# A cross-attention, attention and mixture-of-experts layer: the weight split moved into the second walk, the replicating loads cut in two halves by heads

## The reference

```python
def reference(x, ctx, ...):
    x = x + xattn(layernorm(x), ctx, Wq, bq, Wk, bk, Wv, bv, Wo, bo)
    return x + block(layernorm(x), ...)

def block(x):                                   # x: (8, 512, 256), float32
    q, k, v = heads(x @ wq), heads(x @ wk), heads(x @ wv)        # 16 heads of 16
    attn = softmax(causal(q @ k.T / 4))
    h = x + rmsnorm((attn @ v) @ wo, attn_norm_w)
    dense = h + rmsnorm((silu(h @ w1) * (h @ w3)) @ w2, ff_norm_w)
    probs = softmax(x @ router_w)
    topw, topi = top_k(probs, 2)
    sparse = rmsnorm(sum(topw * expert(topi, x)), moe_norm_w)
    return dense + sparse
```

## Time and profile before

| | us |
|---|---|
| median of three runs | 1455.98 (1455.1 to 1457.37) |
| the profiled execution | 1460.08 |
| its span | 1458.3 |
| PE busy | 1329.9 (91%) |
| DVE busy | 816.3 (56%) |
| ACT busy | 561.9 (39%) |
| POOL busy | 607.0 (42%) |
| mean granted TensorE clock | 0.969 |

### The profile page before, as it was taken

How to read it: one execution, slowest core, us unless ns; L and a number is a source line. 1 busy time by engine, 2 the same in 40 slices (tenths; PEclk the granted TensorE clock), 3 DMA queues, 4 the chain that set the end, 5 groups by cost and what they waited for, 6 DMA issues and landing times. The chain is left out here.

```text
span 1458.3 us, 21947 instructions
## 1 busy us (share of the span) xinstructions
PE 1329.9 (91%) x6989; PEld 848.7 (58%) x6990; DVE 816.3 (56%) x1672; ACT 561.9 (39%) x1191; POOL 607.0 (42%) x1040
## 2 busy tenths in 40 slices
PE   7998839999989999999999899989999889999995
PEld 5454415665666466556647665665666346666674
DVE  3444825476458546754864585368547633333348
ACT  2333226404531651264055316512640634444446
POOL 5112107234522742372354326423622445555544
PEclk9998969999999999999999999999999999999997
DMA  6138530350062008003500620080032434422245
GB/s 217 51 102 281 188 116 1 94 152 17 1 165 82 16 26 221 17 1 97 150 16 0 180 68 16 28 218 16 1 102 74 154 115 130 130 86 85 86 195 188
DMA packets 82264, 141.61 MB, mean 97 GB/s; under 512 B 10632, under 2 KB 66336, under 8 KB 78720
## 3 DMA queue, kind: packets, MB, share of 16 engines
q1 hardware_dynamic: 62512, 94.37, 21.2%
q10 hardware_dynamic: 13184, 28.34, 6.6%
q0 software_dynamic: 6480, 17.77, 3.5%
HBM read 84.90 MB, written 55.15 MB: 96 GB/s over the span
## 5 line engine op out<-in xcount | busy, mean ns | idle before, releaser
L1620 DVE TENSOR_REDUCE nm<-ps 128x2 f32<-128x256 f32 (+3 forms) x256 | 200.7, 820 | 50.5 <-PE ps L1001 46.6
L1290 ACT ACTIVATE room<-ps 128x512 f32<-128x512 f32 x320 | 177.0, 599 | 99.3 <-PE ps L1027 99.1
L1082 PE MATMUL ps<-hT,w 128*128 128x512 f32 x768 | 210.3, 418 | 0.0
L691 POOL TENSOR_SCALAR_AFFINE_SELECT room<-room 128x256 f32<-128x256 f32 (+1 forms) x320 | 133.4, 430 | 127.5 <-ACT room L1290 122.5
L1082 PEld LDWEIGHTS ps<-hT,w 128*128 128x128 f32 x768 | 144.0, 193 | 34.1 <-issue 0.6
L929 PE MATMUL ps<-room,xnT 128*128 128x512 f32 x256 | 129.9, 632 | 29.6 <-ACT xnT L1177 29.6
L1000 PE MATMUL ps<-room 96*128 96x128 bf16 (+3 forms) x512 | 122.6, 308 | 31.9 <-DMA room<-parts_d 22.3
L1118 PE MATMUL ps<-room 128*128 x284 | 135.4, 599 | 1.9 <-ACT room L1340 1.9
L1312 ACT ACTIVATE room<-ps 128x512 f32<-128x512 f32 x64 | 37.9, 594 | 253.8 <-PE ps L1082 253.8
L1092 PE MATMUL ps<-w,room 128*128 128x256 f32 x512 | 129.9, 390 | 3.0 <-DVE room L1671 2.9
L951 PE MATMUL ps<-room 128*128 128x256 f32 x512 | 123.3, 384 | 0.0
(11 more groups left out here) (246 smaller groups left out, 2265.1 us busy)
## 6 DMA issues: line engine op xcount, KB each, us to landing
room<-parts_d ACTq DMA_DIRECT2D x48, 256.0 KB, 6.2
room<-parts_d SPq DMA_DIRECT2D x48, 256.0 KB, 9.6
room<-xs_d SPq DMA_DIRECT2D x71, 129.0 KB, 2.1
parts_d<-room SPq DMA_DIRECT2D x64, 128.0 KB, 1.7
vw_d<-stage ACTq DMA_DIRECT2D x8, 1024.0 KB, 6.3
room<-pair_d SPq DMA_DIRECT2D x8, 1024.0 KB, 8.0
m_d<-stage ACTq DMA_DIRECT2D x8, 896.0 KB, 6.2
room<-m_d SPq DMA_DIRECT2D x7, 1024.0 KB, 5.1
```

The lines of the kernel that those rows point to most:

```text
L691: done(g.affine_select(out=w, in_=w, compare_op=ALU.is_ge, fill=0.0, base=0, pattern=[[0, 2]] * (blocks - 1) + [[1, P]], channel_multiplie ...
L1082: last = mm(bank(up_banks(b, m)[i]), w[:, x, k, m * P:(m + 1) * P], hT[:, y, k, :], start=((x, y, k) == terms[0]), stop=((x, y, k) == term ...
L1290: done(fn(prob[:, u * 512:(u + 1) * 512], bank(score_bank(b) + n % 2), ACT.Exp), "b_exp")
L1620: done(v.tensor_reduce(nm[:, t, 2 * hp:2 * hp + 2], pair_ps, AX.X, ALU.max, negate=True), "a_max")
```

## The change

**The split.** `w_split` leaves the first walk. In the second walk (and in no other) four pieces of it, each for one of w1 and w3 and one half of the rows, stand at four places among the score units. The inputs move to the start of `room`, over `m_first`, `vw_first` and what the second walk uses later (`hT`, `th`, `gT`), so ACT's turn of h and PE's first product with w1 now wait for all four pieces. SP issues the loads of w1 and w3 at the same place of its sequence, with a wait on `sc_ps` for those on `q_out` and `scat`. DVE's first score addition waits for the split no more.

**The loads.** Each of the twelve loads becomes two of 128 KB, for heads 0 to 7 and 8 to 15. Heads stand in `q_rep` and `k_rep` in their natural order now (`rep_at` goes; the columns of wq and wk are reordered for it by four copies in place of two). ACT issues the six first halves of the queries, SP the six of the keys; SP then waits for `q_out` and issues all twelve second halves (`rep_late`) before the load of the next x. `max.0.0` waits for the first halves; `max.4.0`, the first of head 8, waits for `rep_late`. SP's next m load waits for `rep_late` as well.

```diff
-    max.6.1 max.6.2 max.6.3 vf.7.0 nx_apply max.7.0 max.7.1 vf.7.1 max.7.2 vw_out.5 vw_out.6 max.7.3 vw_out.7 shift_parts.1 z w_split
+    max.6.1 max.6.2 max.6.3 vf.7.0 nx_apply max.7.0 max.7.1 vf.7.1 max.7.2 vw_out.5 vw_out.6 max.7.3 vw_out.7 shift_parts.1 z
...
+    sc.1.0 sc.1.1 va.0.1 sc.1.2 sc.1.3 va.0.2 sc.1.4 ct.0.0 sc.1.5 cs.2.0 sc.1.6 sc.1.7 ct.0.1 out_t.0 sc.1.8 sc.1.9 w_split.0.0 va.1.0 va.1.1 exp.1 sc.2.0 x_bias
+    sc.2.1 sum.1 cs.2.1 sc.2.2 va.1.2 sc.2.3 sc.2.4 w_split.0.1 cv.0.0 exp.2 sc.2.5 sc.2.6 cv.0.1 out_t.1 va.2.0 cs.3.0 sum.2 ct.1.0 ct.1.1 sc.2.7 sc.2.8 cs.3.1
+    sc.2.9 sc.3.0 w_split.1.0 cv.1.0 sc.3.1 sc.3.2 ct.2.0 va.2.1 sc.3.3 sc.3.4 exp.3 f_hb cv.1.1 va.2.2 sum.3 sc.3.5 ct.2.1 sc.3.6 w_split.1.1 va.3.0 sc.3.7 cv.2.0 sc.3.8
...
-        w13_in = [part(11264 + i * KD * FF, KD * FF).rearrange("p (k n) -> p k n", k=KD) for i in range(2)]
+        w13_in = [part(i * KD * FF, KD * FF).rearrange("p (k n) -> p k n", k=KD) for i in range(2)]
...
                     for j in range(NREP):
-                        src = parts_d[K_PART[j], 1, :, :, :, :].rearrange("d h a n -> d (h a n)")
-                        done(sp.dma_start(k_rep[j:KREP:NREP, :, :].rearrange("d h n -> d (h n)"), src), "rep_k", 16)
+                        src = parts_d[K_PART[j], 1, :, 0:H // 4, :, :].rearrange("d h a n -> d (h a n)")
+                        done(sp.dma_start(k_rep[j:KREP:NREP, 0:H // 2, :].rearrange("d h n -> d (h n)"), src), "rep_k", 16)
+                    need(sp, b, "q_out", per["q_out"])
+                    for part_of, side, rep in ((K_PART, 1, k_rep), (Q_PART, 0, q_rep)):
+                        for j in range(NREP):
+                            src = parts_d[part_of[j], side, :, H // 4:, :, :].rearrange("d h a n -> d (h a n)")
+                            done(sp.dma_start(rep[j:KREP:NREP, H // 2:, :].rearrange("d h n -> d (h n)"), src), "rep_late", 16)
                     if not (isinstance(b, int) and b == B - 1):
                         load_x(b + 1)
                     if c is not None and b != B - 1:
                         need(sp, b, "rep_q", per["rep_q"])
                         need(sp, b, "rep_k", per["rep_k"])
+                        need(sp, b, "rep_late", per["rep_late"])
...
                     if c is None:
-                        need(sp, b, "q_out", per["q_out"])
+                        need(sp, b, "sc_ps", per["sc_ps"])
                         need(sp, b, "pv_ps", per["pv_ps"])
-                        need(sp, b, "scat", per["scat"])
...
+                        if nmax == per["a_max"] // 2:
+                            need(pe, b, "rep_late", per["rep_late"])
...
+                    elif kind == "w_split" and c == 0:
+                        i, k = step[1:]
                         act.wait_ge(p0["w_up"], 32)
-                        for w, src in zip((w1, w3), w13_in):
-                            fn(w[:, 0, :, :], src, ACT.Copy).then_inc(p0["split_hi"], 1)
+                        fn((w1, w3)[i][:, 0, k, :], w13_in[i][:, k, :], ACT.Copy).then_inc(p0["split_hi"], 1)
...
                     elif kind == "f_h_turn":
+                        if c == 0:
+                            act.wait_ge(p0["split"], 4)
...
-                            if c == 0:
-                                dve.wait_ge(p0["split"], 2)
...
+                    elif kind == "w_split" and c == 0:
+                        i, k = step[1:]
+                        dve.wait_ge(p0["split_hi"], 2 * i + k + 1)
+                        w = (w1, w3)[i]
+                        v.tensor_tensor(w[:, 1, k, :], w13_in[i][:, k, :], w[:, 0, k, :].bitcast(F32), ALU.subtract).then_inc(p0["split"], 1)
```

More of the change, by code:

```diff
@@ L56 @@
     qk_ps=4, part1=4, rest1=4, part2=4, part3=4, v_ps=4, v_sb=4, lg=4,
-    q_out=96, k_out=96, rep_q=96, rep_k=96, z=1,
+    q_out=96, k_out=96, rep_q=96, rep_k=96, rep_late=192, z=1,
     gmax=1, gexp=1, mask=1, rank_ps=1, slot=1, xk=1, scat=128, dve_step=42, pool_a=4, pool_n=1,
@@ L154, in score_bank @@
     return 2 if b is None else 6
-def rep_at(h):
-    return h % (H // KD) * KD + h // (H // KD)
 def score_rows(u):
@@ L447, in send_shifts @@
                 for r in range(MROWS):
-                    done(sp.dma_start(q_rep[KREP + r:KREP + r + 1, rep_at(first_head):rep_at(end_head - 1) + 1:KD, :],
+                    done(sp.dma_start(q_rep[KREP + r:KREP + r + 1, first_head:end_head, :],
                                       mT[r * H + first_head:r * H + end_head, i, :]), f"m_row{i}", 16)
@@ L961, in batch @@
                                 pe.wait_ge(p0["w_late"], 16 * 9)
-                                pe.wait_ge(p0["w_turned"], 2)
+                                pe.wait_ge(p0["w_turned"], 2 * KD)
                             need(pe, b, "xn2T", 2)
@@ L999, in batch @@
                             o = nmax % 2 * 2 + i
-                            mm(bank(o, n), q_rep[0:KREP, rep_at(h), t * P:n], k_rep[0:KREP, rep_at(h), 0:n], start=True, stop=False)
+                            mm(bank(o, n), q_rep[0:KREP, h, t * P:n], k_rep[0:KREP, h, 0:n], start=True, stop=False)
                             last = mm(bank(o, P, t * P), ident_b[:, :], mask_qk[:, :], start=False, stop=True)
@@ L1025, in batch @@
                             o = (score_bank(b) + n % 2) * 512 + at
-                            h = rep_at(4 * grp + j)
+                            h = 4 * grp + j
                             last = mm(ps[:, o:o + S - kb * P], k_rep[0:KREP + MROWS, h, kb * P:(kb + 1) * P], q_rep[0:KREP + MROWS, h, kb * P:S],
@@ L1071, in batch @@
                             if c == 0:
-                                pe.wait_ge(p0["split"], 2)
+                                pe.wait_ge(p0["split"], 4)
                         elif m == 1:
@@ L1223, in batch @@
                         act.dma_start(vw_d[:, :, :, 2 * pa:2 * pa + 2, :].rearrange("c b k j m -> (b k) c (j m)"), vw_stage[pa % 4]).then_inc(kv_out[pa % 4], 16)
-                    elif kind == "w_split":
+                    elif kind == "w_split" and c == 0:
+                        i, k = step[1:]
                         act.wait_ge(p0["w_up"], 32)
-                        for w, src in zip((w1, w3), w13_in):
-                            fn(w[:, 0, :, :], src, ACT.Copy).then_inc(p0["split_hi"], 1)
+                        fn((w1, w3)[i][:, 0, k, :], w13_in[i][:, k, :], ACT.Copy).then_inc(p0["split_hi"], 1)
                     elif kind == "x_turn":
@@ L1279, in batch @@
                         for j in range(NREP):
-                            src = parts_d[Q_PART[j], 0, :, :, :, :].rearrange("d h a n -> d (h a n)")
-                            done(act.dma_start(q_rep[j:KREP:NREP, :, :].rearrange("d h n -> d (h n)"), src), "rep_q", 16)
+                            src = parts_d[Q_PART[j], 0, :, 0:H // 4, :, :].rearrange("d h a n -> d (h a n)")
+                            done(act.dma_start(q_rep[j:KREP:NREP, 0:H // 2, :].rearrange("d h n -> d (h n)"), src), "rep_q", 16)
                         need(act, b, "gmax", 1)
@@ L1548, in batch @@
                         for i, w in enumerate((wq, wk)):
-                            v.tensor_copy(w[:, :, :].rearrange("p k (a d h) -> p (k a) d h", a=KD, d=HD),
-                                          w_heads[:, i, :, :].rearrange("p k (a h d) -> p (k a) d h", a=KD, d=HD)).then_inc(p0["w_turned"], 1)
+                            for a in range(KD):
+                                v.tensor_copy(w[:, :, a * P:(a + 1) * P].rearrange("p k (d h) -> p k d h", d=HD),
+                                              w_heads[:, i, :, :].rearrange("p k (h a d) -> p k a d h", a=KD, d=HD)[:, :, a, :, :]).then_inc(p0["w_turned"], 1)
                         for w in (aw_bc, fw_bc, mw_bc):
                             v.tensor_scalar(w[:, :], w[:, :], float(D) ** 0.5, None, ALU.mult).then_inc(p0["w_turned"], 1)
-                        dve.wait_ge(p0["w_turned"], 5)
+                        dve.wait_ge(p0["w_turned"], 2 * KD + 3)
                     elif kind == "norm_3":
@@ L1592, in batch @@
                                 done(v.tensor_tensor(maskb[:, :, :], mask1, mask2, ALU.add), "mask")
-                    elif kind == "w_split":
-                        for i, (w, src) in enumerate(zip((w1, w3), w13_in)):
-                            dve.wait_ge(p0["split_hi"], i + 1)
-                            v.tensor_tensor(w[:, 1, :, :], src, w[:, 0, :, :].bitcast(F32), ALU.subtract).then_inc(p0["split"], 1)
+                    elif kind == "w_split" and c == 0:
[3 more added lines that the diff above has]
+                        v.tensor_tensor(w[:, 1, k, :], w13_in[i][:, k, :], w[:, 0, k, :].bitcast(F32), ALU.subtract).then_inc(p0["split"], 1)
                     elif kind == "slots":
```

3 lines of the change are left out of this document (removed).

## The result

The changed kernel takes 1401.49 us (median of four runs, 1398.16 to 1406.19), against 1456.67 us of the kernel before beside it (four runs, 1455.1 to 1459.28): a ratio of 0.962, 95% interval 0.959 to 0.966. On another chip it took 1403.99 (six runs, 1397.6 to 1407.2) against 1455.99 (eleven runs), 0.963 [0.959, 0.966]. The forecast was 1399 us, the range 1391 to 1415.

A forecast was written before the change was run, and what follows sets the result against it. TensorE, busy 91% of the span, was taken as the bound through its waits. Gains 24.1 + 3.0 - 0.7 + 22.3 + 9.3 - 0.8 = 57.2 us cut the span from 1458.3 to 1401.1; forecast 1399 us, range 1391 to 1415.

The forecast's parts named there:

- the gap at the second walk: Before the second walk, PE's 24.9 us wait for ACT's copy of xnT falls to 0.8; gain 24.1 us.
- lead of the second walk: cold start less split and two loads: Second walk's start to PE's first maximum: 3.0 us gained without cold start, less 0.2 for pieces, 0.5 for loads.
- waits for the loads: PE's eight waits for replicated queries and keys at the first maximum vanish with halved loads; gain 22.3 us.
- half clock behind them: TensorE at 1.2 instead of 2.4 GHz after load waits in first, second, third, seventh, eighth walks goes; gain 9.3 us.
- half clock at walk boundaries: Half clock follows short gaps at half of seven walk boundaries, 6.0 us against 5.2 now; 0.8 us lost.
- rival (a): In the second walk PE waits for every piece of the split; 8 us more, 1407 us; chance 8%.
- (b): Second walk stalls some 5 us on w1 and w3 or shift rows, then 1.7 us half clock; 1406 us; 7%.
- can't pass: On SP's queue shift rows can't overtake the 2 MB of w1 and w3; 0.5 us for both loads, otherwise 0.2.
- (d): Replicating loads cost 1.38 us per load, not per byte, so halving removes no wait; 1431 to 1444 us; 8%.
- (e): Twelve halves take longer than twelve wholes, late ones hold PE at head 8; slower, up to 1496 us; 3%.
- Rival (c): At the first maximum DVE's slots come 1 us after PE in each walk; 8 us, 1407 us; chance 4%.
- From the span to the runs: The runs' median was taken to stand 4.1 us under the profiled execution, as before: 1402.9 gives 1399 us.

The follow-up runs named there:

- the turned order: The changed kernel with SP issuing the w1 and w3 loads behind the three shift-row loads instead of ahead; one execution took 1400.81 us.
- the later second piece: The changed kernel with the split's second piece moved behind sum.2; 1400.4 us in one execution, then timed at 1403.78 us, ratio 0.963 to the kernel before.
- the four pieces: The changed kernel with all four pieces of the split at the first of their places, ahead of exp.1; one execution took 1411.47 us.
- the wait for all: The changed kernel with the first maximum waiting for the late halves too, loads unmoved; 1426.95 us, ratio 0.979 to the kernel before.

## Why the prediction was right

| term | forecast | measured |
|---|---|---|
| the gap at the second walk | 24.1 | 24.1 (24.92 - 0.78) |
| lead of the second walk: cold start less split and two loads | 3.0 - 0.7 = 2.3 | 92.12 - 90.01 = 2.1 |
| waits for the loads | 22.3 | 23.6 |
| half clock behind them | 9.3 | 10.0 |
| half clock at walk boundaries | -0.8 | +0.5 |
| sum | 57.2 | 60.3 (spans) |

**The gap** came as forecast, down to the 0.78 us that remain.

**The split** has about the right size and a wrong reason. I gave the four pieces 0.2 us and the two loads 0.5. The loads cost nothing: w3 landed at 191.81, 0.9 us before ACT came to the first piece (192.71, 19.3 us into the walk, as forecast), and the shift rows at 192.37, 1.3 us before sc.2.0 at 193.63. The order of the queue is as I had it, and as the Trainium skill has it in "DMA: Bandwidth & Descriptors", section "Queues, rings and completion order"; the experiment with the turned order shows it in numbers. That section speaks of the order in which descriptors are consumed and says that a later one may still finish first, so my "can't pass" was more than it states; here nothing passed. The pieces cost 0.90 us in place of 0.2, through an engine that I hadn't looked at for this part, POOL: I had asked whether ACT and DVE have the time, not what else slows down while DVE subtracts. The sign of rival (a), a longer lead of that walk alone, is there, at a ninth of its price; (b) is out. The four copies for wq and wk, which I had put at nothing, cost 0.2 us at most: the first walk's lead is 96.12 us, and it was 95.94.

**The loads.** The first halves were to land 9.2 us after the first issue and 4.8 us ahead of PE. They land after 8.9 to 9.3 us in the walks two to eight, 4.6 to 5.1 us ahead of PE's arrival, and 3.7 us ahead in the first walk. The late ones were to have 10 us of room at head 8 and have 11 to 14. SP's twelve go out in 7.59 us and the x load at 390.88, 87.8 us into the walk; I had put it at 430 - 342.3 = 87.7. Rivals (d) and (e) are out: from the second walk on 24 halves take no longer than 12 wholes, so there is next to no cost per load. (The fit that I set beside (e) is for DMAs that GpSimd issues, as its section's title says; these are issued by SP and ACT, and 24 in 15.8 us are 0.66 us each.) The waits brought 1.3 us more than their 22.3, because the first maximum now starts 0.16 us before the product ahead of it has drained, eight times. Rival (c) is out by little: the slots end at 391.89, 0.12 us before the first maximum, and PE's first weight load did wait for them while the product ahead still ran. They are what comes next.

**The half clock behind the waits** was read rightly from the tails: 2.7, 1.6, 1.5 and 1.6 us in the second, third, seventh and eighth walk, as forecast. In the first, where I took 1.8 of 0 to 2.5, it was 2.8 (2.6 in the sum, because the lead ahead of it grew by 0.2). I had let DVE's 3.60 us hold PE up there, and they didn't: what took PE 6.18 us takes 3.37 now.

**The boundaries** were the term that I couldn't fix. Three of seven carry half clock here; over six profiles with the same 0.78 us gap (the change twice, the later second piece twice, the four pieces, the turned order) it was 20 of 42, in other walks each time. The share that I took, a half, holds; which ones it is remains open.

**From the span to the runs** is the step that failed. I took the 4.1 us by which the median of before stood under its profiled execution as fixed. After, the median (1401.49) stands 1.7 us above the profiled execution (1399.8). The sum was 3.1 us short and this step 5.8 us off the other way: the two errors cancel in part, and the forecast is 2.5 us under the median by that luck, nearer than this step deserves. (The low end of the range, by its own terms, is 1391.6.)

## What to carry to other kernels

Let a wait ask only for the data that its first user reads. Cutting the transfers did little by itself (some 7 us, with intervals that overlap), and letting the first products go on the first half did the rest (22 to 25 us); the second half came 11 us or more before it was wanted. Work that is moved under another engine's shadow has to be cut to the size of the gaps there (four pieces of 1 us cost 0.9 us, one block of 4 us cost 4), and each piece has to be looked at for what it slows next to it, not only for the time of its own engine. And a wait of PE can cost more than its length: some 13 of the 60 us here (10.0 behind the loads, 3.0 behind the long gap) are products that run at 2.4 GHz again.

## What the runs showed of the hardware

DVE's subtractions and POOL's work hold each other up whole. The group of DVE's L1527 in the changed kernel (ns, least, median and most of 32):

```profile
L1527 DVE TENSOR_TENSOR room<-room,cmax x32: 1224/1226/2295, 45.2 to 988.8; 128x1024 f32<-128x1024 f32 x32
```

In the rows shown for the second piece, POOL's multiplication ends at 200.06; L1527, begun at 198.85, ends 1.1 us after that, at 201.14, and takes 2.29 us in place of 1.23. POOL's cut, begun at 200.00, ends 0.15 us after L1527; the next, begun at 201.25, ends 0.15 us after DVE's L1600. With DVE idle such a cut takes 0.29 us (36 of them in the changed kernel), and 0.30 beside DVE's reduction L1526, which reads one operand (at 197.88). The Trainium skill, "SBUF — State Buffer", section "SBUF: two separate sides", says that the port pair which DVE and GpSimd share is an exclusive lock, held for a whole instruction by whichever begins first, and that a DVE instruction with two inputs in SBUF takes it against a GpSimd instruction that reads SBUF. The trace agrees: each of these instructions ends just after the one that it had to wait for. It is nothing peculiar to the split: in every walk from the third to the eighth one L1527 takes 2.05 to 2.07 us under POOL's multiplication and the cut behind it 1.3 us, without a wait of PE.

Half clock followed waits of PE of 2.17 us (the four pieces) and 1.82 us (the fifth walk of the wait for all), did not follow one of 2.05 us in the same run (its sixth walk), and followed the short gaps at walk boundaries (0.73, 0.48 and 0.78 us at the second walk) in 20 of 42 cases. It cost 1.5 to 1.7 us in these cases, and 2.3 to 2.4 in two second walks. The length of a wait alone doesn't decide it. In the kernel before it followed one of 1.96 us (the eighth walk, whose tail ran at 0.96) and not one of 2.97 us (the sixth, with its tail at clock 1.00):

```profile
1099.75 0.22 PE L1000 MATMUL ps<-room 96*128 96x128 bf16 x1 [1.96 <-DMA room<-parts_d]
...
833.30 0.22 PE L1000 MATMUL ps<-room 96*128 96x128 bf16 x1 [2.97 <-DMA room<-parts_d]
...
833.30:873.14 39.84, 37.08 (x233) 26.65 (x233) 35.65 (x65) 5.16 (x14) 12.64 (x13) 1.00 0.32 95
```
